# Channel norm: 1/sd is widened on GpSimd, y is added to x during the first convolution, weight levels go through int32, and fewer constant matmuls stand ahead of batch norm 1

## What is computed

```python
y = _ln_c(x)                                   # (x - mean) / sqrt(var + 1e-6) over the 64 channels
m = pat.astype(jnp.float32)                    # a 3 x 3 pattern of zeros and ones
out = conv3x3(quant_act(batchnorm(y, gamma1, beta1)), quant_weight(w1) * m)
out = conv3x3(quant_act(batchnorm(out, gamma2, beta2)), quant_weight(w2) * m)
x = x + (out + y)
t = _to_tokens(x)
t = t + ffn(_ln_t(t), router_w, w1, w2, w3)    # 8 experts, the best 2 for each token
# quant_weight(w): t = tanh(w) / (2 max|tanh(w)|) + 0.5;  2 * round(15 t) / 15 - 1
# quant_act(x):    round(15 * clip(x, 0, 1)) / 15
```

## Time and profile before

| what | value |
|---|---|
| median of 3 runs | 842.06 us (838.06 to 842.35) |
| the profiled execution: first to last instruction | 838.0 us |
| its mean granted PE clock | 0.949 of full speed |
| busy: PE, DVE, ACT, POOL | 774.5, 562.4, 491.8, 540.8 us |
| channel norm and batch norm 1, up to the start of convolution 1 | 0 to 62.2 us |
| convolution 1 | 62.2 to 94.7 us |

### The profile page before, as it was taken

The page is one execution under the profiler, slowest core; times in us unless marked ns, Lnnn a source line. Parts: engine busy times, 40 slices in busy tenths (PEclk is TensorE's granted clock), DMA queues, the critical chain, the costliest instruction groups (busy, mean ns, idle before and its releaser), DMA issues.

```text
span 838.0 us, 17914 instructions
## 1 busy us (share of the span) xinstructions
PE 774.5 (92%) x5003; PEld 444.2 (53%) x5007; DVE 562.4 (67%) x1462; ACT 491.8 (59%) x1071; POOL 540.8 (65%) x564
## 2 busy tenths in 40 slices
PE   8979978886899999999999999999999999999834
PEld 6744465564354545454545455454545457777523
DVE  5976678888566666666666666666767566666445
ACT  5836458775166666666666666666666566666400
POOL 3520027777777777777777777777777777777610
PEclk9969989897999999999999999999999999999955
DMA  8760023343244443333334343433333346666179
GB/s 197 138 111 1 0 62 102 115 136 110 80 131 134 123 122 115 112 116 112 114 113 121 108 124 106 129 112 116 113 114 115 104 134 183 185 180 185 62 273 327
DMA packets 84227, 105.55 MB, mean 126 GB/s; under 512 B 27061, under 2 KB 57966, under 8 KB 84176
## 3 DMA queue, kind: packets, MB, share of 16 engines
q1 hardware_dynamic: 60688, 79.27, 32.5%
q0 software_dynamic: 19136, 21.54, 9.1%
q10 hardware_dynamic: 4352, 4.20, 1.5%
HBM read 73.90 MB, written 27.30 MB: 121 GB/s over the span
## 4 chain that ended last, share of the span: by engine, by line
PE 80%; DVE 8%; issue 4%; DMA 3%; SPq 2%; ACT 2%; DVEq 0%; POOL 0%; POOLq 0%; ACTq 0%
PE bank L1432 40%; PE bank L1447 22%; PE bank L1312 6%; PE bank L1413 3%; DMA conv_all<-result_rows 2%; PE bank L1405 2%; SPq L492 1%; PE bank L1234 1%; PE bank L1247 1%; PE bank L1252 1%; PE bank L1263 1%; PE bank L1337 1%; PE bank L1330 1%; DMA x_all<-in_x 1%; DVE stats L1011 1%
## 5 line engine op out<-in xcount | busy, mean ns | idle before, releaser
L553 POOL DMA_INDIRECT expert_rows<-y_and_rows,slot_all x256 | 249.4, 974 | 144.2 <-issue 77.1
L1165 DVE TENSOR_TENSOR conv_all<-conv_all,bank 128x512 f32<-128x512 f32 x340 | 233.6, 688 | 151.5 <-ACT conv_all L747 149.2
L1432 PE MATMUL bank<-xT,w 64*128 64x512 f32 (+1 forms) x1608 | 324.7, 534 | 0.4 <-DVE conv_all L1165 0.4
L747 ACT ACTIVATE conv_all<-bank 128x512 f32<-128x512 f32 x340 | 203.2, 598 | 117.0 <-PE bank L1432 117.0
L1432 PEld LDWEIGHTS bank<-xT,w 64*128 64x128 f32 x1608 | 143.7, 185 | 170.3 <-DVE conv_all L1165 86.2
L563 POOL DMA_INDIRECT result_rows<-conv_all,dest_all x142 | 140.1, 987 | 47.1 <-issue 40.9
L1447 PE MATMUL bank<-conv_all,w 128*64 128x256 f32 x1240 | 161.7, 384 | 1.2 <-DVE tile_map L1134 1.2
L1447 PEld LDWEIGHTS bank<-conv_all,w 128*64 128x64 f32 x1240 | 91.1, 136 | 51.7 <-issue 12.7
L758 ACT ACTIVATE xT<-bank 64x256 f32<-64x256 f32 x272 | 103.3, 380 | 18.6 <-PE bank L1405 16.2
L765 ACT ACTIVATE conv_all<-bank 128x256 f32<-128x256 f32 x68 | 26.2, 385 | 85.6 <-PE bank L1447 85.6
L563 POOL DMA_INDIRECT result_rows<-squares,dest_all x64 | 63.2, 987 | 19.5 <-issue 18.6
(11 more groups left out here) (247 smaller groups left out, 882.9 us busy)
## 6 DMA issues: line engine op xcount, KB each, us to landing
w<-expert_w SPq DMA_DIRECT2D x68, 384.0 KB
w<-expert_w SPq DMA_DIRECT2D x68, 192.0 KB
conv_all<-expert_rows SPq DMA_DIRECT2D x56, 136.0 KB
x_all<-in_x SPq DMA_DIRECT2D x16, 256.0 KB, 4.0
x_all<-y_and_rows POOLq DMA_DIRECT2D x16, 256.0 KB, 4.3
expert_rows<-y_and_rows,slot_all POOLq DMA_INDIRECT x256
y_and_rows<-result_rows SPq DMA_DIRECT2D x8, 512.0 KB, 10.2
conv_all<-result_rows SPq DMA_DIRECT2D x8, 512.0 KB, 11.0
```

Source lines behind the costliest of these rows:

```text
L553: nc.gpsimd.indirect_dma_start(xs, bass.IndirectOffsetOnAxis(ap=slot_all[:, s, k * GH + g:k * GH + g + 1], axis=0), rows_all[:, s, g, :], ...
L747: nc.scalar.activation(sbuf[k % 3], h1_ps[k % 3][:], ACT.Silu).then_inc(silu_rdy, 1)
L1165: V.tensor_tensor(hbuf[k], sbuf[k % 3], h3_ps[k % 3][:], ALU.mult).then_inc(mul_rdy, 1)
L1432: ins = mm(ps[k % 3][:, rows_], w[half, cols], xT[u][half, rows_], start=True, stop=True)
```

## The change

Four edits. First, DVE no longer widens 1/sd: POOL does, as `widen(p)`, with a wait for the last step of `rstd(p)` and for the transposes of the pair before; PE's `spread` waits for POOL instead of DVE. Second, all sixteen `residual` transfers stand behind the eighth `widen` in POOL's list. Third, the convolution weights are rounded by one ACT pass that writes int32, and two DVE instructions (`odd_levels`, behind `stats0(2)` and `stats0(3)`) take 7.5 off, multiply by twice the pattern and write bf16; POOL's product and four steps of ACT go, the copy is no longer doubled, and `blocks` reads the same 64 rows twice. Fourth, `keep_busy` is 2 and 20 matmuls around `pair_up(0)`, not 10 and 18.

```diff
-            made(nc.gpsimd.tensor_copy(patf[:], pati[:]))
+            nc.gpsimd.tensor_scalar(patf[:], pati[:], 2.0, None, ALU.mult).then_inc(pat_rdy, 1)
...
-            for s in range(4):
+            def widen(p):
+                pool.wait_ge(ln_steps, 4 * p + 4)
+                pool.wait_ge(bc_rdy, 2 * p + 2)
+                nc.gpsimd.tensor_copy(wide[:], st[:, 2, :].unsqueeze(2).broadcast_to([128, GP, C])
+                                      ).then_inc(rstd_rdy, 1)
+
+            for p in range(NP):
+                widen(p)
+            for s in range(NS):
                 residual(s)
-            pool.wait_ge(wq_rdy, 4)
-            wv = wc[:].rearrange("o k (i t) -> o (k i) t", t=TAPS)
-            nc.gpsimd.tensor_tensor(wv, wv, patf[:].unsqueeze(1).broadcast_to([C, 2 * C, TAPS]),
-                                    ALU.mult).then_inc(wmask_rdy, 1)
-            for s in range(4, NS):
-                residual(s)
...
+                    ins = nc.scalar.activation(wlev[:], wc[:], ACT.Copy, scale=LEVELS)
...
             def spread(p):
                 c = ln.begin(p, 4)
                 dve.wait_ge(sd_rdy, 2 * p + 2)
+                if p:
+                    dve.wait_ge(rstd_rdy, p)
                 rstd(c)
-                dve.wait_ge(bc_rdy, 2 * p + 2)
-                V.tensor_copy(wide[:], st[:, 2, :].unsqueeze(2).broadcast_to([128, GP, C])).then_inc(rstd_rdy, 1)
                 c.end()
...
+            def odd_levels(k):
+
+                dve.wait_ge(wq_rdy, 2)
+                dve.wait_ge(pat_rdy, 1)
+                V.scalar_tensor_tensor(wodd[:, k].rearrange("o t i -> o i t"),
+                                       wlev[:, k, :].rearrange("o (i t) -> o i t", t=TAPS), -0.5 * LEVELS,
+                                       patf[:].unsqueeze(1).broadcast_to([C, C, TAPS]),
+                                       ALU.add, ALU.mult).then_inc(wmask_rdy, 1)
...
-            keep_busy(10, bank[2])
+            keep_busy(2, bank[2])
             pair_up(0)
-            keep_busy(18, bank[2])
+            keep_busy(20, bank[2])
```

More of the change, by code:

```diff
@@ L117, in conv_moe_kernel @@
         pati = sb("pat_i", [C, TAPS], I32)
-        wdup = sb("conv_w_dup", [C, 2, TAPS, 2, C], BF16)
+        wlev = sb("conv_w_levels", [C, 2, C * TAPS], I32)
+        wodd = sb("conv_w_odd", [C, 2, TAPS, C], BF16)
         wblk = sb("conv_w_blocks", [128, 2, TAPS, 128], BF16)
@@ L220, in conv_moe_kernel @@
         sd_rdy = sem("sd_ready")
-        rstd_rdy = sem("rstd_ready")
+        ln_steps = sem("vector_layernorm")
+        rstd_rdy = sem("rstd_widened")
         bc_rdy = sem("rstd_spread_ready")
@@ L230, in conv_moe_kernel @@
         wrec_rdy = sem("wmax_reciprocal_ready")
+        pat_rdy = sem("pattern_doubled")
         wmask_rdy = sem("conv_w_masked")
@@ L614, in levels @@
                         ins = nc.scalar.activation(wc[:, k, :], wc[:, k, :], ACT.Copy, bias=0.5, scale=wrec[:, k:k + 1])
-                elif n == 1:
+                else:
                     act.wait_ge(wq_rdy, 1)
[L617 to L629, removed]
+                    ins = nc.scalar.activation(wlev[:], wc[:], ACT.Copy, scale=LEVELS)
                 ins.then_inc(wq_rdy, 1)
@@ L633, in blocks @@
                 act.wait_ge(wT_rdy, k + 1)
-                turned = w_bf[k].rearrange("p (t c) -> p t c", t=TAPS)
-                nc.scalar.activation(wblk[0:64, k, :, 0:64], turned[0:64], ACT.Copy)
-                nc.scalar.activation(wblk[64:128, k, :, 64:128], turned[64:128], ACT.Copy).then_inc(wb_rdy, 1)
+                turned = w_bf[k][0:C].rearrange("p (t c) -> p t c", t=TAPS)
+                for h in range(2):
+                    ins = nc.scalar.activation(wblk[64 * h:64 * h + 64, k, :, 64 * h:64 * h + 64], turned, ACT.Copy)
+                ins.then_inc(wb_rdy, 1)
             square(0, 0)
@@ L650, in _ @@
                     centred(p + 2)
-                if p < 6:
+                if p < 2:
                     levels(p)
@@ L864, in rstd @@
                 c(V.scalar_tensor_tensor(r, w, 1.5, r, ALU.add, ALU.mult))
-            ln = chain("vector_layernorm")
+            ln = Chain()
+            ln.sem = ln_steps
             def variance(p):
@@ L903, in _ @@
                 stats0(p - 1)
+                if p in (3, 4):
+                    odd_levels(p - 3)
             norm(NP - 1, 0)
@@ L907, in _ @@
             dve.wait_ge(st_rdy, NS)
+            dve.wait_ge(bc_rdy, NS + 2)
             V.memset(hbuf[HT], 0.0)
@@ L1277, in turn_conv_weights @@
             def turn_conv_weights(k):
-                pe.wait_ge(wq_rdy, k + 5)
+                pe.wait_ge(wmask_rdy, k + 1)
                 for t in range(TAPS):
-                    ins = nc.tensor.transpose(w_bf[k][:, C * t:C * t + C],
-                                              wdup[:, k, t, :, :].rearrange("o d i -> o (d i)"), ident_bf[0:C, 0:C])
+                    ins = nc.tensor.transpose(w_bf[k][0:C, C * t:C * t + C], wodd[:, k, t, :],
+                                              ident_bf[0:C, 0:C])
                 ins.then_inc(wT_rdy, 1)
```

## The result

| | before | after |
|---|---|---|
| median of 7 runs | 839.39 us (838.06 to 842.35) | 844.72 us (844.01 to 845.97) |
| the profiled execution, first to last instruction | 838.0 | 842.1 |
| mean granted PE clock in it | 0.949 | 0.942 |

The ratio is 1.0057, interval 1.0042 to 1.0072: slower, by a little over 0.5%. 844.72 lies inside the predicted range, but on the wrong side of no change, and inside only because the range was built on a median of three runs, 842.06, that lies 2.7 us above the median of seven: luck.

The account below looks back on a forecast made before the run. PE was taken to bound the channel norm, DVE close behind. pair_up(0) starts 3.8 us earlier, 2.2 are given back at the lower clock, so convolution 1 starts 1.6 earlier: 842.06 - 1.6 = 840.5 us, range 836.5 to 845.0.

Parts of the forecast that it names:

- POOL's copy: Widening of 1/sd in the channel norm: 1.13 us on POOL (bounds 0.90 to 2.22), costing nothing up to pair 5.
- The tail: Last channel-norm pairs, a loop through PE, DVE and the copy: stage ends 1.3 us earlier, moments at 53.43.
- The transfers: Sixteen y-into-x transfers behind POOL's eighth copy: issued by 65.7, landed by 72.9, 29 us before the first reader.
- rival 4: The sixteen transfers come late: at 3.7 us each the last lands 12 us late, 852.6 us; chance 0.05.
- three signs named for being wrong: POOL's copy over 2 us, DVE's norm longer than 0.69 beside it, or the clock's rise after the twenty constants.
- The weights: Two DVE instructions on 64 x 576 in the channel norm: 0.77 us each, 1.25 at most, hidden by PE's 4.33 round.
- rival 1: PE's clock rises later, so 20 constants ahead of convolution 1 take 8.5 us, ending 62.45: 842.3 us; chance 0.13.
- Everything behind convolution 1's start moves along.: After convolution 1's start: the later kernel shifts with it, so its 1.6 us earlier start counts in full.
- rivals 2 and 3: 2: PE's clock back at once, 838.1 us, chance 0.10. 3: POOL's copy slow or holding norm, 842.5 or 846, 0.12.
- The base: Starting time for the sum: median 842.06 us, with the lowest run 0.06 above the profiled span of 838.0.

Follow-up runs that it names:

- layout_it: Changed kernel with the odd-levels tile laid out taps inside, so L889 reads and writes in order and PE's transposes read strided: 842.85 us, ratio 1.0022.
- weights_only: layout_it with 1/sd widened on DVE again, each transfer sent once its stripe is there, and 10 and 18 constant matmuls: 840.12 us, ratio 0.9999.
- loop_order: Changed kernel with L889 looping taps outside, channels inside, so it writes bf16 in order and reads int32 strided: 841.67 us, ratio 1.0007.
- after_fill: Changed kernel with 15 more constant matmuls in the first routing pair, where PE waited for DVE: 842.0 us, ratio 1.0019.
- layout_fill: layout_it with 15 more constant matmuls in the first routing pair, where PE waited for DVE: 838.72 us, ratio 0.9972.
- before_fill: Kernel before the change with the same 15 constant matmuls in the first routing pair: 838.46 us, ratio 0.9986.

## Why the prediction was wrong

**Right.** POOL's copy: 1.040 us for 1.13, `norm` beside it 0.69, no cost in pairs 1 to 3, no 1.80 us L862 any more. The Trainium skill, SBUF — State Buffer, Who interferes with whom, has a VectorE instruction with one SBUF input not blocked; the trace agrees. The estimate of 1.54 us for the copy, from the Trainium skill, GPSIMD Engine Reference, Performance versus the Vector engine, was too high; the row decides. The tail: with quick weights (layout_it) the way from `spread(1)` to `spread(7)` is 1.4 shorter (25.44 to 24.00), forecast 1.16 there and 1.3 at the moments (its own steps end at 51.60, not at 51.7); of it weights_only has 0.9 (24.57), and POOL's widening the other 0.5. The transfers: landed by 76.6 for 72.9, a little past the 75 of the forecast, as one took 18.2 us to land; convolution 1 to the first slots is unchanged at 56.57, so the cover held and rival 4 did not come. None of the three signs named for being wrong came; the signs that spoke were the idle time ahead of `spread(4)` and `pair_up(0)` 2.3 us late.

**The first step that failed: "The weights".** "The nearest row, 128 x 512 with two inputs in 0.68, gives 0.77; at the rate of POOL's product it would be 1.25 ... hidden by PE, and 0.3 late in two rounds at the upper price." It measured 2.34 to the next instruction, because the nearest row writes in memory order and this one doesn't; so the bound was not a bound. DVE's round became 4.00 - 0.61 + 2.34 = 5.73, above PE's 4.33. `spread(4)` idled 0.38, the clock fell at 37.56, `centred(7)` lost 1.55, and `pair_up(0)` came at 55.85, not 53.5. Convolution 1 missed 60.68 by 2.46 us: with the rise at 58.84 the 20 matmuls from 56.30 would have ended at 58.84 + 14 x 0.217 = 61.88, 1.2 late for `pair_up`'s sake; the rise at 61.45 gave the other 1.26. So a part of rival 1 came, a later rise, but behind a late `pair_up(0)`; with quick weights (layout_it) the rise is at 59.14, near the 58.84 of the forecast.

**The second: "Everything behind convolution 1's start moves along."** It doesn't. The routing pair, 57 us later, lost 3.6 us, since PE's clock went down in the same pause for 13.65 us instead of 6.83. With the first step mended (layout_it) convolution 1 started 0.3 from the forecast, and the kernel still measured 1.0022. No rival held this step: rival 1 spoke of the clock, but ahead of convolution 1, and rivals 2 and 3 are refuted by the rise and by the copy.

**What each step was worth in whole times.** The changed kernel stands at 1.0057. L889 in order brings it to 1.0022 (layout_it; loop_order 1.0007), the filled pause alone to 1.0019 (after_fill), both to 0.9972 (layout_fill). The same fill brings the kernel before to 0.9986 (before_fill), so it also takes away what the pause cost before. Set against that, the loss of 4.8 us (0.0057 of 840) parts so: 2.8 are left with the pause filled in both kernels (1.0019 against 0.9986), so the second step cost 2.0; mending L889 as well gives back 3.9 (0.9972), the cost of the first; and the kernel is then 1.2 us faster than the kernel before with the same fill, near the forecast 1.6, though the two intervals overlap. Either step alone takes the gain away.

**The base.** The runs' times are 1.7 to 2.9 us above their spans, 1.9 in the middle. So the "lowest run 0.06 above" the profiled span said nothing about it, and 838.0 stands for some 839.9, not 842.06. A sum made on that would have been 838.3.

**Left open.** Why a pause of the same 3.8 us goes with 3.41 us at the lower level in one profile and with 13.65 in another is not shown; shown is that the start of convolution 1 beside the rise goes with it in nine of ten profiles without the fill, one for each kernel, that it doesn't need the changed kernel, and that the pause filled removes it. That the start sets it, rather than something that differs from run to run, is argued and not shown. Open too is why the second step cost 2.0 us in whole times and 3.6 in the profiles, and why L889 is worth 3 to 4 us, where convolution 1, counted from `spread(1)`, starts only 2.0 to 2.5 us later by it there (37.90 and 39.86 with the fill, 37.34 and 39.87 without). Why strided writes cost this much is not shown either. The late transfers alone were not tried.

## What to carry to other kernels

Price a DVE instruction from a row whose access order is the same, not only its size: 64 x 576 took 0.73, 1.16 or 2.7 us by that alone. Before a stretch is taken to move along unchanged, look also far behind the edit for pauses in which PE's clock goes down: 15 constant matmuls in one were worth about 3 us to the changed kernel (1.0057 to 1.0019), 4 to layout_it and 1 to the kernel before. And useful work can take the place of constants that stand ahead of the clock's rise: with 10 fewer ahead of convolution 1 the rise came no later from `pair_up(0)` on, and the ratio fell from 0.9972 to 0.9945 (the ends of the intervals just meet).

## What was not expected of the hardware

Strided bf16 writes on DVE: 2.73 us against 0.73 in order. PE's transposes paid for the other layout, though little: nine with a strided read took 1.24 for 0.69 at the lower clock. In layout_it DVE waits for them, by way of ACT's `blocks` and L1302, 0.36 us ahead of the moments:

```profile
52.54 0.16 DVE L915 COPY router_T<-bank 64x8 f32<-64x8 f32 x1 [0.36 <-PE bank L1302]
```

And the same pause of PE went with 3.41 to 13.65 us of lower clock, by how far behind the rise convolution 1 had started. Sixteen transfers issued by POOL without a break landed in up to 18.2 us each, yet all were done within 27 us of the first issue at 50.07.
